# An RK4 scan on one core: the second evaluation's linear part moves from TensorE to VectorE

## The reference, cut to what matters

```
def _derivative(q, p, drive, coupling, bias):
    i_couple = jnp.tanh(q) @ coupling.T
    dq = q - q ** 3 / 3.0 - p + drive + i_couple + bias
    dp = EPSILON * (q + ALPHA - BETA * p)
    return (dq, dp)
def _rk4_step(q, p, drive, coupling, bias):
    dq1, dp1 = _derivative(q, p, drive, coupling, bias)
    dq2, dp2 = _derivative(q + 0.5 * DT * dq1, p + 0.5 * DT * dp1, drive, coupling, bias)
    dq3, dp3 = _derivative(q + 0.5 * DT * dq2, p + 0.5 * DT * dp2, drive, coupling, bias)
    dq4, dp4 = _derivative(q + DT * dq3, p + DT * dp3, drive, coupling, bias)
    q_next = clip(q + DT / 6.0 * (dq1 + 2 * dq2 + 2 * dq3 + dq4), -CLAMP, CLAMP)
    p_next = clip(p + DT / 6.0 * (dp1 + 2 * dp2 + 2 * dp3 + dp4), -CLAMP, CLAMP)
```

## Time and profile before

| | us |
|---|---|
| Median of 3 runs | 923.74 (923.41 to 925.33) |
| Profiled execution, its time | 922.4 |
| Its span, first to last instruction | 920.7 |
| Mean granted TensorE clock, share of full speed | 0.992 |
| RK stage, first E1 to the end | from 726.05 |
| PE busy over the span | 901.2 (98%) |
| DVE busy over the span | 615.9 (67%) |

### The profile page before, as it was taken

One profiled execution on the slowest core, in us unless ns is written; L12 is line 12 of the kernel. 1 busy time (PEld: TensorE's weight loads), 2 busy tenths in 40 slices (PEclk: granted clock), 3 DMA queues, 4 the chain that ended last, 5 costly groups with the idle time before them and its releaser, 6 DMA issues.

```text
span 920.7 us, 18591 instructions
## 1 busy us (share of the span) xinstructions
PE 901.2 (98%) x7254; PEld 771.7 (84%) x7254; DVE 615.9 (67%) x1706; ACT 414.4 (45%) x1147; POOL 260.0 (28%) x344
## 2 busy tenths in 40 slices
PE   8999999999999999999999999999998999999998
PEld 6778888888888888888877778999975699999997
DVE  6544555644565644656578875777777888888887
ACT  3233322343222432224346654555544766666665
POOL 0655500011000300015202434333214643333333
PEclk9999999999999999999999999999998999999999
DMA  8122000000000000110022000000000000000000
GB/s 302 58 64 87 24 1 1 2 1 1 2 1 1 1 1 1 46 47 1 1 90 105 1 1 0 2 1 1 2 1 1 1 1 25 1 24 2 24 2 24
DMA packets 5432, 22.01 MB, mean 24 GB/s; under 512 B 608, under 2 KB 736, under 8 KB 4960
## 3 DMA queue, kind: packets, MB, share of 16 engines
q1 hardware_dynamic: 5344, 20.82, 6.5%
HBM read 18.72 MB, written 2.10 MB: 23 GB/s over the span
## 4 chain that ended last, share of the span: by engine, by line
PE 87%; DVE 8%; ACT 3%; issue 1%; POOL 0%; POOLq 0%; DVEq 0%; ACTq 0%
PE ps L355 43%; PE ps L742 8%; PE ps L746 6%; PE ps L610 6%; PE ps L432 6%; PE ps L741 5%; PE ps L600 3%; PE ps L612 3%; PE ps L421 2%; PE ps L617 1%; DVE g_lo L1209 1%; DVE m_lo L1203 1%; PE ps L367 1%; DVE frs L1181 1%; PE ps L362 1%
## 5 line engine op out<-in xcount | busy, mean ns | idle before, releaser
L1126 DVE TENSOR_SCALAR qk<-ps,vec 128x512 f32<-128x512 f32 x64 | 47.9, 749 | 100.0 <-PE ps L355 99.9
L355 PE MATMUL ps<-x_hi,W_hi 128*128 128x512 f32 x256 | 102.0, 399 | 0.7 <-DVE x_lo L1254 0.4
L809 ACT ACTIVATE qk<-ps,vec 128x512 f32<-128x512 f32 x64 | 44.2, 690 | 125.6 <-PE ps L355 125.6
L355 PE MATMUL ps<-x_hi,W_lo 128*128 128x512 f32 x256 | 99.8, 390 | 0.0
L355 PE MATMUL ps<-x_lo,W_hi 128*128 128x512 f32 x256 | 99.8, 390 | 0.0
L742 PE MATMUL ps<-rk_th,cpc 128*128 128x128 f32 x512 | 98.6, 295 | 1.0 <-ACT rk_th L1075 0.6
L1137 DVE SCALAR_TENSOR_TENSOR o_lo<-ps,vec,o_hi 128x512 fp32r<-128x512 f32 x64 | 47.1, 744 | 72.6 <-ACT o_hi L825 69.1
L825 ACT ACTIVATE o_hi<-ps,vec 128x512 fp32r<-128x512 f32 x64 | 44.0, 688 | 111.9 <-PE ps L432 111.9
L742 PEld LDWEIGHTS ps<-rk_th,cpc 128*128 128x128 f32 x512 | 72.2, 191 | 9.9 <-ACT rk_th L1075 7.5
L741 PE MATMUL ps<-rk_th,cpc 128*128 128x64 f32 x512 | 78.4, 255 | 0.0
L610 PE MATMUL ps<-ht,hh 128*128 128x128 f32 x512 | 77.1, 283 | 0.8 <-DVE ht L1464 0.7
(11 more groups left out here) (257 smaller groups left out, 2143.5 us busy)
## 6 DMA issues: line engine op xcount, KB each, us to landing
stage<-qkv_w SPq DMA_DIRECT2D x6, 768.0 KB, 4.4
stage<-out_w SPq DMA_DIRECT2D x4, 512.0 KB, 3.9
f_raw<-ffn_w SPq DMA_DIRECT2D x2, 1024.0 KB, 4.9
xorig<-xT SPq DMA_DIRECT2D x1, 2048.0 KB, 8.4
out<-xtb SPq DMA_DIRECT2D x4, 512.0 KB, 3.1
x_all<-xT SPq DMA_DIRECT2D x1, 1536.0 KB, 15.4
ada_sb<-ada_w SPq DMA_DIRECT2D x1, 1024.0 KB, 9.8
BD<-qkv_w SPq DMA_DIRECT2D x1, 768.0 KB, 6.2
```

Of the source, the lines that this page charges most:

```text
L355: r = pe.matmul(out_, lhsT, rhs, start=first and i == 0, stop=last and i == n - 1)
L809: act.activation(qk[:, 0, h % 2, :], ps[:, PJ[0], :], ACT.Identity, bias=col("qkv_b", HU * u + h)).then_inc(act_evac, 1)
L1126: dve.tensor_scalar(qk[:, 1, h % 2, :], ps[:, PJ[1], :], col("qkv_b", HEADS + HU * u + h), None, ALU.add).then_inc(dve_evac, 1)
```

## The change

The first evaluation is as it was. For the second, PE no longer multiplies Z2 with the identity: a new function `chunks_alone` starts both banks with the first tanh product and finishes them together. DVE subtracts Z2 from w instead (a new instruction, y2, in place in w), and then subtracts that from the banks. Z2 moves behind q2, t3 moves from behind q2 to the place behind U2, s1 moves behind q3, and s2 and s3 move one place back each. On ACT V4 and V5 change places (V4 ahead of the first tanh, V5 behind the second square). The function `linear` and the streams of POOL and of the DMA queues stay as they are.

```
--- before.py
+++ after.py
@@ -70,11 +70,11 @@
            "z_h1", "zc_n1", "h1")
 GRU_ACT = ("r0", "z0", "zc0", "n0", "r1", "zc1", "z1", "n1")
 GI_STEPS = (4, 9, 13, 18, 22, 27, 31, 36)
-RK_ACT = ("V5", "th1a", "th1b", "sq1", "V4", "th2a", "th2b", "sq2", "th3a", "th3b", "sq3", "Da", "Db", "th4a", "th4b",
+RK_ACT = ("V4", "th1a", "th1b", "sq1", "th2a", "th2b", "sq2", "V5", "th3a", "th3b", "sq3", "Da", "Db", "th4a", "th4b",
           "sq4", "V3")
-RK_DVE = ("q", "U2", "Z2", "w1", "q2a", "q2b",
-          "t3", "s1", "Z3", "w2", "q3a", "q3b",
-          "s2", "Z4", "s3", "w3", "q4a", "q4b",
+RK_DVE = ("q", "U2", "t3", "w1", "q2a", "q2b",
+          "Z2", "Z3", "w2", "y2", "q3a", "q3b",
+          "s1", "Z4", "s2", "w3", "s3", "q4a", "q4b",
           "s4", "P", "w4", "E1", "qa", "qb")
 RK_POOL = ("store", "U4", "m", "b4", "U3")
 POOL_DVE = ("score_vec", "wo_sum", "wqr", "wo_mean", "wo_c", "scaled06", "resid06", "score06", "max06", "scaled7", "resid7", "score7", "score_max", "score_sub",
@@ -758,6 +758,15 @@
                 coupled(k, 1, 0, False, False)
                 coupled(k, 1, 1, False, True).then_inc(rk_pe, 1)
 
+            def chunks_alone(t, k):
+                pe.wait_ge(rk_dve, RK_START + at(t, RK_DVE, "q2b"))
+                tanh_done(t, k, "a")
+                coupled(k, 0, 0, True, False)
+                coupled(k, 1, 0, True, False)
+                tanh_done(t, k, "b")
+                coupled(k, 0, 1, False, True).then_inc(rk_pe, 1)
+                coupled(k, 1, 1, False, True).then_inc(rk_pe, 1)
+
             def chunks_together(t, k):
                 tanh_done(t, k, "a")
                 coupled(k, 0, 0, False, False)
@@ -770,9 +779,7 @@
                 pe.wait_ge(rk_dve, RK_START + at(t - 1, RK_DVE, "E1") if t else RK_START)
                 linear(1, "E1")
                 chunks_together(t, 1)
-                pe.wait_ge(rk_dve, RK_START + at(t, RK_DVE, "Z2"))
-                linear(2, "Z2")
-                chunks_in_turn(t, 2)
+                chunks_alone(t, 2)
                 pe.wait_ge(rk_dve, RK_START + at(t, RK_DVE, "Z3"))
                 linear(3, "Z3")
                 chunks_together(t, 3)
@@ -1079,13 +1086,13 @@
 
                 if t:
                     dve_done("P", t - 1)
-                scaled("V5", K5)
+                scaled("V4", K4)
                 tanhs(1, "qraw", t - 1, ("qa", "qb"))
                 dve_done("q")
                 square("q", C_ / 3)
-                scaled("V4", K4)
                 tanhs(2, "q2", t, ("q2a", "q2b"))
                 square("q2", C_ / 3)
+                scaled("V5", K5)
                 tanhs(3, "q3", t, ("q3a", "q3b"))
                 square("q3", 2 * C_ / 3)
                 drive(t + 2)
@@ -1605,8 +1612,9 @@
                 else:
                     inc(dve.tensor_copy(r_["q"], r_["qraw"]))
                 inc(STT(r_["U2"], r_["P"], -K2, r_[f"D{t % 3}"], M, Ad))
-                mine("U2")
-                inc(STT(r_["Z2"], r_["q"], 1 - A_ * C_, r_["U2"], M, Ad))
+                pool("U3", t - 1)
+                mine("q")
+                inc(STT(r_["t3"], r_["q"], 0.5, r_["U3"], M, Ad))
                 act_done("sq1")
                 inc(STT(r_["w"], r_["qsq"], -(C_ + 1), r_["q"], Ad, M))
                 a1 = coupling(1, 0)
@@ -1614,26 +1622,30 @@
                 inc(dve.tensor_tensor(half("q2", 0), a1, half("w", 0), Su))
                 inc(dve.tensor_tensor(half("q2", 1), coupling(1, 1), half("w", 1), Su))
 
-                pool("U3", t - 1)
-                inc(STT(r_["t3"], r_["q"], 0.5, r_["U3"], M, Ad))
-                inc(STT(r_["s1"], r_["q"], W1, r_["V5"], M, Ad))
-                mine("t3")
+                mine("U2")
+                inc(STT(r_["Z2"], r_["q"], 1 - A_ * C_, r_["U2"], M, Ad))
+                mine("q2b")
                 inc(STT(r_["Z3"], r_["q2"], -A_ * C_, r_["t3"], M, Ad))
                 act_done("sq2")
                 inc(STT(r_["w"], r_["qsq"], -C_, r_["q2"], Ad, M))
+                mine("w2")
+                inc(dve.tensor_tensor(r_["w"], r_["w"], r_["Z2"], Su))
                 a2 = coupling(2, 0)
-                mine("w2")
+                mine("y2")
                 inc(dve.tensor_tensor(half("q3", 0), a2, half("w", 0), Su))
                 inc(dve.tensor_tensor(half("q3", 1), coupling(2, 1), half("w", 1), Su))
 
+                act_done("V5")
+                inc(STT(r_["s1"], r_["q"], W1, r_["V5"], M, Ad))
                 pool("b4")
-                inc(STT(r_["s2"], r_["q2"], W2, r_["s1"], M, Ad))
                 mine("q3b")
                 inc(STT(r_["Z4"], r_["q3"], 2 * (1 - A_ * C_), r_["b4"], M, Ad))
+                mine("s1")
+                inc(STT(r_["s2"], r_["q2"], W2, r_["s1"], M, Ad))
+                act_done("sq3")
+                inc(STT(r_["w"], r_["qsq"], -2 * C_, r_["q3"], Ad, M))
                 mine("s2")
                 inc(STT(r_["s3"], r_["q3"], W3, r_["s2"], M, Ad))
-                act_done("sq3")
-                inc(STT(r_["w"], r_["qsq"], -2 * C_, r_["q3"], Ad, M))
                 a3 = coupling(3, 0)
                 mine("w3")
                 inc(STT(half("q4", 0), a3, 2.0, half("w", 0), M, Su))
```

## The result

| | before | changed |
|---|---|---|
| Median | 924.65 us (6 runs, 923.41 to 927.33) | 942.06 us (6 runs, 940.59 to 943.2) |
| Ratio, 95% interval | | 1.0184, 1.0165 to 1.0202 |
| Profiled execution, its time | 922.4 | 940.59 |
| Its span | 920.7 | 938.5 |
| Usual distance of two clips of q | 5.87 | 6.35 |

The kernel became slower, as forecast (938.7), but by 2.4 us more over its own base than I said, and outside the range (931 to 941). The forecast, 938.7 over a base of 923.74, is a ratio of 1.0162.

The account below looks back on a forecast made before the run. It took the RK step for a latency loop (q2, tanh, products, q3), not PE-bound. 31 distances at +0.50, with first-step, long-addition and rounding corrections, gave 922.4 + 15.0 = 937.4 profiled, plus 1.3: 938.7 us; range 931 to 941.

Parts of the forecast that it names:

- t3 held by the store: DVE, middle step: t3, now ahead of w1, is blocked by POOL's store, costing 0.16 us on the path.
- t3 escapes: Rival: t3 is not held by POOL's store, y2 still is by b4; +0.30 a step, 932.5 us; 11%.
- Z2 and Z3 free, no gain from PE's freed loads: Z2 and Z3 behind q2 cost nothing; PE's four freed loads, 0.45 to 0.53 us, gain 0 because products wait for tanh.
- PE-bound rival: Rival: PE sets the pace, so four loads fewer each step save 14.4 us, giving 909.3; 4%.
- y2: DVE, second evaluation: y2 is held by POOL's b4, costing 0.09; q3's chunks come at 2.90 and 3.04.
- rival of the literal rule: Rival: t3 and y2 start only at POOL's full end, 0.13 more each, 946.8 us; 3%, shared with another new wait.
- The order of the products: PE, second evaluation, chunks_alone: q3's chunks ready at 2.72 and 2.94, before DVE needs them, so no cost.
- The step: Middle RK step, one clip of q to the next: 6.37 us for 5.87, +0.50.
- without y2's: Rival: y2 is not held by POOL but t3 is; +0.41 a step, 935.8 us; 5%.
- without both: Rival: neither t3 nor y2 is held; +0.20 a step from the longer chain w2, y2, q3; 930 us; 8%.
- the two long additions: Two steps with a long POOL addition, where Z4 was held 0.47 before: -0.35 us each.
- The first step, "+0.33": First RK step has no store to hold t3, so it lengthens by only 0.33 us.

Follow-up runs that it names:

- e2: Changed kernel with t3 moved back behind q2, so it no longer starts beside POOL's store: 934.47 us, ratio 1.0094.
- e3: Changed kernel with Z2 in PSUM, so that y2 has one SBUF input: 938.59 us, ratio 1.0128.
- e5: Kernel before with only evaluation 2's product order changed to chunks_together, Z2 still summed on PE: 929.16 us, ratio 1.0049.
- e8: Kernel before, unedited, timed and profiled again: 924.91 us, ratio 1.0003.
- e1: Changed kernel, unedited, timed and profiled again: 941.17 us, ratio 1.0156.
- e12: Changed kernel, unedited, timed a third time, on the same chip as a version with added idle PE products: 940.26 us, ratio 1.0164.
- e6: Kernel before with one edit, DVE forms Z2 behind w1 and not ahead of it: 923.37 us, ratio 0.9988.
- e7: Changed kernel plus 16 fillers (PE products nobody reads) in the first RK step ahead of evaluation 2: 937.94 us, ratio 1.0152.
- e9: Kernel before with 64 fillers (PE products nobody reads) ahead of the RK stage, not 40: 924.06 us, ratio 0.9987.
- e10: Kernel before with Z2 behind w1 and 64 fillers ahead of the RK stage, not 40: 921.86 us, ratio 0.9967.
- e11: Changed kernel with 64 fillers ahead of the RK stage, not 40, and 16 in its first step: 940.12 us, ratio 1.0153.
- e13: Changed kernel with 64 fillers ahead of the RK stage and 16 in its first step, timed again beside the unedited one: 938.05 us, ratio 1.0160.

## Why the prediction was right, and where it was wrong

1. *t3 held by the store*: right. 0.57 for 0.57, w1 at 0.83, q2 at 1.22 and 1.36. e2 takes the hold away and gets 0.174 a step, and the 9th step against a usual one shows the same inside one kernel. The rival "t3 escapes" happened in three steps of 31, where POOL's extra wait turns the order round; I had not read that wait.
2. *Z2 and Z3 free, no gain from PE's freed loads*: right. PEld idles 0.85 where I said over 0.5. The PE-bound rival, read from the chain's 87%, is out: four loads a step went and nothing came back.
3. *y2*: right. 0.38 for 0.37, q3 at 2.89 and 3.03 for 2.90 and 3.04. e3 has the hold at 0.10, for 0.09. The rival of the literal rule, blocked to POOL's full recorded end (946.8), is out: t3 and y2 end 0.14 and 0.15 behind that end, as the earlier trace rows had it.
4. *The order of the products*, left at nothing: right. PE was to have q3's chunks at 2.72 and 2.94 and DVE to decide at 2.90 and 3.04; neither chunk waits for PE in the step above. e5's 0.14 is what the order costs where PE decides.
5. *The step*: 6.37 said, 6.35 measured. The prices of the rivals came out too: without t3's hold +0.31 (said 0.30), without y2's +0.38 (0.41), without both +0.21 (0.20). The thirty distances grew by 14.13, for the 14.3 of the sum (30 x 0.50 less 0.7). That this is so near is in part luck: the step was 0.48 longer and not 0.50 (-0.6), the two long additions gave back 0.56 and not 0.7 (+0.1), the three escapes were not in the sum (-0.5), and there are 0.8 more of late steps than before had.
6. *The first step, "+0.33"*: wrong, and this is the step of the forecast that failed. It measured +3.2 between the two profiles: 2.6 for a dip of 6.8 us, 0.13 for E1's hold, and 0.47 for the rest, where U2's hold makes the difference to 0.33. The sum went from one execution of before whose first step had no dip and the shortest E1 of all; e8 shows that kernel with 8.86, 0.92 of it by a dip and 0.74 by E1. The clock was among my rivals only as a fall for the whole stage, at 2%, with +5 a step. The exchange of V4 and V5 stood at nothing as "two like scalings"; in a usual step this was right, in the first it brought U4 beside U2.
7. *What makes the dip* is not shown. It stood in the first step in ten of the eleven profiles with 40 fillers (6.8 us in the first of the changed kernel, e1, e12 and e2 to e6; 3.4 in e7 and e8; none in the first of before) and in none of the four with 64 (e9, e10, e11, e13). PE had been idle ahead of the first product with E1 for 1.31 to 2.20 us in the ten, 1.18 in the first of before, and 0.24 to 0.88 in the four. The lost products with Z2 are not needed for it (e5, e6).
8. *The base*: before's median moved from 923.74 (3 runs) to 924.65 (6 runs), 0.9 us; in all comparisons its runs went from 922.07 to 930.01. Part of this spread may be the same dip, so it is not to be added to item 6. Taken as ratios, the forecast's 1.0162 lies just under the interval of the first comparison (1.0165 to 1.0202) and within those of e1 and e12 (measured 1.0156 and 1.0164), and e12's 940.26 us lies inside the range. A range that ended 2.3 above the forecast had no room for that spread.

What stays open: what the late steps are (same places with the same instructions, other places when t3 moves; in the 3rd, q3's first chunk waits 0.46 for PE, where it does not wait in a usual step), how often the dip falls and what brings it on, and where the 0.4 us outside the span come from.
